# A written table of slots in place of computed positions, in an attention and expert layer

## The reference

```
xn = _layernorm(x)
x = x + attn(xn, ...) + ffn(xn, ...)

attn, for each of 16 heads of 16 numbers:
  scores = q k^T / 4                       # causal mask
  std    = softmax(scores) v Wo^T
  gsa    = softmax(scores + 0.3 * splat) v Wo^T   # splat: 16 features of q by 16 features of k
  attn   = (1 - blend) * std + blend * gsa

ffn, 16 experts, 2 for each token, room for 128 tokens in each:
  scores = sqrt(softplus(xn gate_w^T)); the two largest of scores + gate_b
  y      = sum over the two: w * W2[e] (silu(W1[e] xn) * (W3[e] xn))
  shared = Ws2 (silu(Ws1 xn) * (Ws3 xn))
```

## Time and profile before

| | |
|---|---|
| median of three runs | 359.38 us |
| lowest, highest | 357.64, 359.58 us |
| the profiled execution's own time | 357.81 us |
| its span, first to last instruction | 356.1 us |
| mean granted TensorE clock | 0.981 of 2.4 GHz |
| PE busy, share | 320.7 us, 90% |
| DVE busy, share | 237.0 us, 67% |
| ACT busy, share | 199.6 us, 56% |

### The profile page before, as it was taken

The page is one execution under the profiler, slowest core; times in us unless marked ns, Lnnn a source line. Parts: engine busy times, 40 slices in busy tenths (PEclk is TensorE's granted clock), DMA queues, the critical chain, the costliest instruction groups (busy, mean ns, idle before and its releaser), DMA issues.

```text
span 356.1 us, 6144 instructions
## 1 busy us (share of the span) xinstructions
PE 320.7 (90%) x2112; PEld 163.8 (46%) x2112; DVE 237.0 (67%) x693; ACT 199.6 (56%) x297; POOL 39.7 (11%) x59
## 2 busy tenths in 40 slices
PE   1989988987879999899999999999999999999984
PEld 1437733332433454444554454445445554445352
DVE  5988585497997668865676657755765568566424
ACT  1567457574635575754655564555556545647730
POOL 7200000000010000111111111102010004444000
PEclk9998999998987999999999999999999999999999
DMA  7423354324136502545465545454554443222011
GB/s 243 131 45 55 58 93 100 60 38 67 20 59 142 113 2 43 125 100 147 99 137 132 162 115 146 114 127 110 132 139 131 109 82 77 62 62 64 9 61 59
DMA packets 25823, 33.56 MB, mean 94 GB/s; under 512 B 4668, under 2 KB 18588, under 8 KB 25788
## 3 DMA queue, kind: packets, MB, share of 16 engines
q1 hardware_dynamic: 24088, 28.85, 35.6%
q0 software_dynamic: 1536, 4.20, 4.2%
q10 hardware_dynamic: 164, 0.07, 0.1%
HBM read 16.15 MB, written 4.26 MB: 57 GB/s over the span
## 4 chain that ended last, share of the span: by engine, by line
PE 45%; DVE 6%; ACT 3%; issue 2%; DVEq 0%
PE ps L914 12%; PE ps L830 7%; PE ps L839 5%; PE ps L896 5%; PE ps L884 4%; PE ps L790 4%; PE ps L869 2%; ACT arena_p L682 2%; PE ps L887 1%; DVE mx L1257 1%; PE ps L834 1%; ACT small L694 1%; PE ps L843 1%; DVE wt L1273 1%; DVE ps L1224 1%
## 5 line engine op out<-in xcount | busy, mean ns | idle before, releaser
L682 ACT ACTIVATE arena_p<-ps 128x1024 f32<-128x1024 f32 (+1 forms) x192 | 148.0, 808 | 52.0 <-PE ps L896 30.5
L1257 DVE TENSOR_REDUCE mx<-ps 128x1 f32<-128x512 f32 (+1 forms) x100 | 60.2, 628 | 20.8 <-PE ps L790 14.2
L914 PE MATMUL ps<-arena_p,v_full 128*32 128x512 f32 (+3 forms) x768 | 74.0, 504 | 0.0
L790 PE MATMUL ps<-stage 96*128 96x512 bf16 (+3 forms) x160 | 49.7, 347 | 7.5 <-DVE mx L1257 3.5
L884 PE MATMUL ps<-stage 98*128 98x512 bf16 (+1 forms) x192 | 51.3, 332 | 4.2 <-ACT arena_p L682 3.0
L896 PE MATMUL ps<-stage 98*128 98x512 bf16 (+1 forms) x192 | 46.8, 332 | 1.9 <-ACT arena_p L682 1.9
L456 POOL DMA_INDIRECT wt<-xn_scratch,ids_sb x16 | 15.3, 957 | 236.8 <-PE ps L818 103.6
L1224 DVE CUSTOM_DVE_ANT_0 ps<-ps,mask_r 128x128 f32<-128x128 f32 (+1 forms) x80 | 38.6, 498 | 2.6 <-PE ps L790 2.5
L914 PEld LDWEIGHTS ps<-arena_p,v_full 128*32 128x32 f32 x768 | 20.3, 110 | 34.9 <-issue 30.4
L790 PEld LDWEIGHTS ps<-stage 96*128 96x128 bf16 x160 | 15.5, 98 | 29.1 <-issue 21.2
L687 ACT ACTIVATE small<-ps 128x176 f32<-128x176 f32 x24 | 7.6, 317 | 37.1 <-PE ps L830 37.1
(11 more groups left out here) (204 smaller groups left out, 387.1 us busy)
## 6 DMA issues: line engine op xcount, KB each, us to landing
w_sb<-in_w_dram SPq DMA_DIRECT2D x16, 352.0 KB
stage<-split SPq DMA_DIRECT2D x48, 96.0 KB, 2.8
stage<-split SPq DMA_DIRECT2D x96, 32.0 KB, 2.3
stage<-split SPq DMA_DIRECT2D x48, 64.0 KB, 2.7
arena_o<-in_w_dram SPq DMA_DIRECT2D x16, 176.0 KB
ye_scratch<-wt SPq DMA_DIRECT2D x16, 128.0 KB, 2.3
stage<-split SPq DMA_DIRECT2D x32, 48.0 KB
acc<-in_x_dram SPq DMA_DIRECT2D x4, 256.0 KB, 3.7
```

The lines of the kernel that those rows point to most:

```text
L682: A(to, ps[:, 1 + 2 * s:3 + 2 * s, off:CH], ACT.Exp, scale=SCALE).then_inc(done, 1)
L790: ins = M(b[:, 0:n1 - n0], qs[0:KR, pr, h, it * P:(it + 1) * P], ks[0:KR, pr, h, n0:n1], start=True, stop=not masked)
L914: ins = M(ps[c:c + 2 * HD, 0, off:CH], v_full[:, jb + s, g * GH + h, :], of, start=jb + s == 0, stop=end or last, skip_group_check=last an ...
L1257: V.reduce_max(to, b[:, 0:n1 - n0], AX.X).then_inc(aux_free, 1)
```

## The change

The functions and lists that compute the positions go, and `PLAN` is written out: eight lists of 24 lists. Every task that stood in the lists before stands in them once; 166 of the 337 keep their slot. Nothing else is changed: what a task does, the waits, the banks' rotation, the fixed work and SP's rows. As banks go by the order of tasks, a task can now wait for another one than before. `AT` (the slot of each task that isn't repeated) is read off the table.

In the table groups differ from each other. Some of what changes:

- Group 0: all eight `pre` maxima stand in slots 0 to 2, both `square` in slot 4, `p0` 4 in slot 5 instead of 8, both `feat1` of the first column half in slot 6 and of the second in slot 10; the ten last maxima stand one by one or in threes between slots 12 and 19; `route` 3 follows `route` 2 in slot 14, `rest` 4 comes in from group 1, `rest` 5 likewise.
- Group 1: `route` 6 in slot 1 and `route` 7 in slot 6, one `max` each in slots 2 to 5, `oT` 1 in slot 7 instead of 3.
- Groups 2 to 5: `shift` 0 in slot 8 or 9, ahead of the maxima of the second half; `max` (0, 5, 1) in slot 10; `xT` of the expert that `gu` takes in slot 22 comes in slot 18 or 19 instead of 20; one maximum at slot 12, 16 and 20; `oT` 1 moves between slots 1 and 4.
- Groups 5 and 6: `hT` in slot 0, `y` in slot 1, `max` (0, 3, 0) only in slot 6 and 5; in group 6 five maxima stand in slot 5 and none in slots 6 and 7.
- Group 7: `out` (6, 0) in slot 9 instead of 10, `oT` 0 in 10 instead of 11, `rows` (1, 0) in 15 instead of 13, `out` (0, 2) in 18 instead of 16, `oTh` 0 in 23 instead of 21; `add` grouped.

The diff, cut:

```diff
-        def slotted(*lists):
-            slots = [[] for _ in range(NSLOT)]
...
-        def spread_late(tasks, first, last):
-            late_slots = [n for n in range(first, last + 1) if n % 4]
-            return [(late_slots[len(late_slots) * n // len(tasks)], t) for n, t in enumerate(tasks)]
...
-        SHARED = ((("sgu", 2), ("shT", 5), ("sy", 6)), (("sgu", 7), ("shT", 9), ("sy", 10)))
-        EXPERT = ((("xT", 0), ("gu", 2), ("hT", 5), ("y", 6)), (("xT", 5), ("gu", 7), ("hT", 9), ("y", 10)))
-
-        maxima = spread_late(max0, 0, 6) + [(9, ("shift", 0))] + spread_late(max1, 7, 20) + [(22, ("shift", 1))]
...
-        AT = {t: at for at, t in long}
-        PLAN = []
-        for g in range(NG):
-            lists = [[(11, ("oT", 0))], [(at - g * NSLOT, t) for at, t in long if at // NSLOT == g]]
...
+        PLAN = [
+            [
+                [("pre", ("max", (1, 4, 0))), ("pre", ("max", (1, 4, 1))), ("pre", ("max", (1, 5, 0))),
+                 ("pre", ("max", (1, 5, 1)))],
+                [("pre", ("max", (1, 6, 0))), ("pre", ("max", (1, 6, 1))), ("pre", ("max", (1, 7, 0)))],
+                [("pre", ("max", (1, 7, 1)))],
+                [("max2", (0,))],
+                [("square", 0), ("square", 1), ("pre", ("shift", 1))],
+                [("max2", (1,)), ("p0", 4), ("max", (0, 2, 0))],
+                [("feat1", (0, 1)), ("feat1", (1, 1)), ("max", (0, 3, 0))],
+                [("max", (1, 2, 0))],
+                [("max", (1, 3, 0)), ("route", 0)],
+                [("p0", 5)],
+                [("max", (0, 4, 0)), ("feat1", (0, 0)), ("feat1", (1, 0)), ("max", (0, 4, 1)), ("max", (0, 5, 0)),
+                 ("max", (0, 5, 1))],
+                [("route", 1), ("oT", 0)],
+                [("shift", 0), ("max", (0, 6, 0))],
+                [("max", (0, 6, 1)), ("max", (0, 7, 0)), ("max", (0, 7, 1)), ("max", (1, 4, 0))],
+                [("max", (1, 4, 1)), ("route", 2), ("route", 3)],
+                [],
+                [],
+                [("max", (1, 5, 0)), ("max", (1, 5, 1)), ("max", (1, 6, 0))],
+                [("max", (1, 6, 1))],
+                [("max", (1, 7, 0)), ("max", (1, 7, 1)), ("rest", 4)],
+                [("route", 4)],
+                [],
+                [("shift", 1)],
+                [("route", 5), ("rest", 5)],
+            ],
+            [
+                [],
+                [("max2", (0,)), ("max2", (1,)), ("route", 6)],
+                [("max", (0, 2, 0)), ("p1", 4)],
+                [("max", (0, 3, 0))],
+                [("max", (1, 2, 0))],
+                [("max", (1, 3, 0))],
+                [("route", 7), ("p1", 5)],
+                [("max", (0, 4, 0)), ("oT", 1)],
...
+                [("max2", (0,)), ("max2", (1,))],
+                [("rest", 6), ("shT", 2), ("rest", 7), ("sy", 2)],
+                [("max", (0, 2, 0))],
+                [("sgu", 3), ("oT", 1), ("max", (0, 3, 0))],
...
+                [("hT", 2), ("xT", 3), ("oT", 1)],
+                [("y", 2), ("max2", (0,))],
+                [("gu", 3), ("max2", (1,)), ("max", (0, 2, 0))],
+                [("hT", 3), ("max", (0, 3, 0))],
+                [("max", (1, 2, 0)), ("max", (1, 3, 0))],
+                [("y", 3)],
+                [("max", (0, 4, 0)), ("max", (0, 4, 1))],
+                [("shift", 0)],
+                [("xT", 4), ("max", (0, 5, 0))],
+                [("max", (0, 5, 1)), ("max", (0, 6, 0))],
+                [("oT", 0), ("gu", 4), ("max", (0, 6, 1))],
+                [("max", (0, 7, 0)), ("max", (0, 7, 1))],
+                [("hT", 4)],
+                [("xT", 5), ("y", 4), ("max", (1, 4, 0)), ("max", (1, 4, 1))],
+                [("gu", 5), ("max", (1, 5, 0))],
+                [("max", (1, 5, 1))],
+                [("hT", 5), ("max", (1, 6, 0))],
+                [("y", 5), ("xT", 6), ("max", (1, 6, 1))],
+                [("max", (1, 7, 0))],
+                [("max", (1, 7, 1))],
+                [],
+                [("gu", 6)],
+                [("shift", 1)],
...
+                [("hT", 10)],
+                [("xT", 11), ("max2", (0,)), ("y", 10), ("max2", (1,)), ("max", (0, 2, 0))],
+                [],
+                [("oT", 1), ("gu", 11)],
+                [],
+                [],
+                [("hT", 11), ("max", (0, 3, 0)), ("max", (1, 2, 0))],
+                [("max", (1, 3, 0)), ("max", (0, 4, 0)), ("y", 11)],
+                [("max", (0, 4, 1)), ("shift", 0), ("max", (0, 5, 0)), ("xT", 12)],
+                [("max", (0, 5, 1)), ("max", (0, 6, 0)), ("max", (0, 6, 1))],
...
+                [("gu", 15), ("oT", 1)],
+                [("hT", 15), ("sgu", 4), ("y", 15)],
+                [("max", (0, 3, 0)), ("max", (1, 2, 0)), ("max", (1, 3, 0)), ("max", (0, 4, 0)), ("max", (0, 4, 1))],
+                [],
+                [],
+                [("shift", 0), ("shT", 4)],
...
+                [("add", (0, 5)), ("out", (4, 0)), ("add", (1, 5))],
+                [],
+                [],
+                [("out", (6, 0))],
+                [("oT", 0)],
+                [],
+                [("add", (0, 6))],
+                [("add", (1, 6)), ("add", (0, 7)), ("add", (1, 7))],
+                [],
+                [("rows", (1, 0))],
+                [],
+                [],
+                [("out", (0, 2))],
+                [("out", (2, 2))],
+                [],
+                [],
+                [],
+                [("oTh", 0)],
+            ],
+        ]
+        AT = {t: g * NSLOT + n for g, slots in enumerate(PLAN) for n, tasks in enumerate(slots) for t in tasks
+              if t[0] not in ("max2", "max", "shift", "pre", "oT")}
```

More of the change, by code:

```diff
@@ L260, in bass_splat_attention_moe_layer @@
-        maxima = spread_late(max0, 0, 6) + [(9, ("shift", 0))] + spread_late(max1, 7, 20) + [(22, ("shift", 1))]
-        LATER = 8
[L262 to L271, removed]
+        LATER = 8
@@ L272, in bass_splat_attention_moe_layer @@
         LAST_FEAT = ("feat1", (1, 0))
-        S_ROUTE, S_SHARED, S_EXPERT, S_ADD = (8, 31), (32, 148), 56, 156
         OWN_AT = (0, 3)
[L275 to L281, removed]
```

124 lines of the change are left out of this document (112 added, 12 removed).

## The result

The changed kernel takes 343.65 us (343.28 to 344.06, four runs) against 358.51 us, the median of the kernel before with a fourth run beside the three. That is a ratio of 0.9585, 95% interval 0.9548 to 0.9622. Forecast were 348.4 us. The profiled execution took 343.76 us with a span of 342.0 us, 14.1 us under the span before.

A forecast was written before the change was run, and what follows sets the result against it. PE was taken as the bound (busy 90%), DVE through group 0 and the start of group 1. Terms -4.5 - 1.0 - 6.0 + 0 - 1.0 + 2.0 = -10.5 us from 357.81, plus 1.1: 348.4 us; range 343 to 354, 356.5 with the DVE case.

The forecast's parts named there:

- Group 0 and the start of group 1, -4.5 us: Group 0 and first third of group 1: DVE's idle time falls from 9.1 to 4.6 us, bounds 0 to -9.1.
- the clock, -1.0 us: Groups 0 and 1: part of the cost of running at 1.2 GHz goes, -1.0 us, bounds +3.4 to -3.4.
- the second stretch: Group 1: 6.8 us at half clock, costing at most 3.4 us; two thirds of that cost was kept.
- Groups 2 to 5, -6.0 us: PE's six short waits mostly go: -1.0, -1.8, -2.2 and -1.0 us by group, bounds 0 to -10.4.
- Group 6, 0: Five maxima in slot 5 cost about 1.3 us, as much as goes at slots 9, 15, 19 and 22; net 0.
- Group 7, -1.0 us: out (0, 2) behind both splats fills the wait of std (5, 0), 0.95 us; rounded -1.0, bounds 0 to -1.5.
- What I can't see, +2.0 us: Groups 1 to 7: new unseen waits, 0.3 us in each of seven groups, +2.0 us, bounds 0 to +8.
- SP, 0: Ahead of max2: slack shrinks about 0.4 us, costed at nothing; rival of late rows, 1 us per group, 352 us, chance 0.08.
- DVE giving the gain back: Rival, first 50 us: DVE's fixed load returns the gain; 353 us, up to 357; chance 0.18.
- The slower side: Clock rival, groups 1, 2, 5, 6: bursts of maxima bring more half-clock stretches, 3.4 us each; 366 us; chance 0.08.
- The sum: Whole kernel: terms add to -10.5 us, 347.3 us; with 1.1 us from profiled execution to the runs, 348.4 us.
- The signs: Group 3 about 2 us shorter, group 0 4 to 5, DVE idle about half, std (5, 0) wait gone, one half-clock stretch in group 1.

The follow-up runs named there:

- a burst: The changed kernel with four maxima of group 0 moved from slots 17 and 18 to slot 15; 350.60 us, ratio 0.9772.
- early maxima: Against the kernel where group 5 was refilled as well: max (0, 3, 0) and max (0, 4, 1) ahead of feat1 in group 0; 340.16 us, ratio 0.9464.
- the third set: Runs on one chip of the kernel where group 5 was refilled as well and three edits of it, beside the kernel before, median 359.9 us.
- the run that shows it alone: The changed kernel with computed slots for groups 5 and 6, the table for 0 to 4 and 7; 341.56 us, ratio 0.9543.
- group 5 was refilled as well: Previous run, but group 5 takes the table's group 4 slots, group 6 maxima, shift and oT as in its group 3; 339.05 us, ratio 0.9473.
- the first kernel: The kernel before with the table for groups 0 and 1 only, computed slots for 2 to 7; 348.83 us, ratio 0.9750.

## Why the prediction was right, and where it was off

The direction and its reasons held, and the time lies in the range; the forecast was 4.7 us too high. By its own steps:

- **Group 0 and the start of group 1, -4.5 us, and the clock, -1.0 us.** Measured -9.3 us for groups 0 and 1. The rule behind the first term is that DVE's idle time counts. Three kernels show it: with a burst, with early maxima and with the table in the middle groups only, group 0 grew by 6.2, 1.7 and 1.3 us where DVE's idle time grew by 6.2, 2.0 and 1.3 us. In the changed kernel it fell from 9.8 to 4.7 us, where 4.6 were worked out; the sum had started from the four longest waits, 9.1 us, and so was 0.7 us short. The step that was mis-sized is the clock. I kept two thirds of the second stretch, since new waits of 2.9 and 1.7 us were to come. They came, as 1.8 and 1.1 us, and where the clock fell with them (the table for groups 0 and 1 alone) it cost nothing, since DVE was busy meanwhile. What the clock took before can be estimated from the kernel before itself: seven of its runs in the third set had a mean clock of 0.971 and a mean of 360.1 us, two had 0.981 and 357.5. A hundredth of 356 us of lost clock is 3.6 us, that is 7.1 us at half speed, for 2.6 us of time, 0.37 us for each. The 10.2 us at half clock in the loop then were worth some 3.8 us, an estimate from these runs, and about 5.5 us were waits. No run has the computed slots of groups 0 and 1 at full clock, so this division isn't shown, nor which moves in group 0 brought its part. One wait of DVE in the second stretch, just behind the window of the earlier trace rows, is gone in the changed kernel:

```profile
108.94 0.69 DVE L1323 COPY pv_sb<-ps 128x512 f32<-128x512 f32 x1 [1.60 <-PE ps L914]
```

- **Groups 2 to 5, -6.0 us.** Measured -2.2 - 1.9 - 2.5 + 0.5 = -6.1 us, by the parts -1.0, -1.8, -2.2, -1.0. For group 5 I was 1.5 us too hopeful: I had seen its wait in slot 8 (0.44 us printed, 0.60 really), not those of `shift` 1 and `std` (6, 0, 0), which stand behind `gu` 14 in slot 21 and start 0.40 and 0.58 us late. For group 2 I was 1.2 us too careful: `oT` 1 didn't wait for the two `rest`s. The slots that I named for groups 2 to 5 are those of groups 3 and 4: in group 5 `max` (0, 5, 1) stands in slot 9, and slots 10 and 12 differ too. The two misses cancel, so it is partly luck that the whole term came out.
- **Group 6, 0.** +1.4 us. The five maxima cost about what was worked out (some 1.1 us by their starts, 276.17 to 278.12 us, the longest wait 0.45 us; 1.3 us were forecast), but `sy` 4 in slot 9 waits another 1.0 us, behind them on DVE, and ACT is late three times.
- **Group 7, -1.0 us.** 1.0 us in the run that shows it alone. The row of `std` (5, 0) has no wait: `splat`s, `out`, `std` follow one another.

```profile
325.18 0.93 PE L1055 MATMUL ps<-stage 98*128 98x512 bf16 x4
325.95 1.89 PE L1028 MATMUL ps<-wt,rest 128*128 128x256 f32 x8
327.68 0.28 PE L1043 MATMUL ps<-stage 98*128 98x256 bf16 x1
```

- **What I can't see, +2.0 us.** Not there in groups 1 to 4, where the measured gains need no such term; in groups 5 and 6 it was, as 2.9 us. Spread over all groups it was the wrong shape: unseen waits stood where the table was dense.
- **SP, 0.** No wait in the changed kernel. Once group 5 was refilled as well, the first showed, with 0.16 us printed.
- **The rivals.** DVE giving the gain back fell with the first kernel: group 2 was 37.7 us long there, as before the change. The slower side fell too: behind group 1 no profiled run shows the half clock, except behind the last matmul of PE. (Its sum comes to 366.5 us, and half of the 10.5 us is 5.3, not 6.) The Trainium skill, "TensorE: Matmul & The Clock Gate", section "A second HAM failure mode: psum-queue depth-cycling", names cycling through PSUM banks as a cause. Six short waits in group 3 before and those between the maxima in group 6 after, of up to 0.45 us, left the clock at 1.00, so here the short waits alone didn't bring it down.
- **The sum.** The span fell by 14.1 us where 10.5 were forecast. The other 1.1 us of the miss is the step from the profiled execution to the median: the changed kernel needed none (343.76 and 343.65 us). The time lies 0.7 us inside the range, near its end.
- **The signs.** The six waits of group 3, the 0.79 us ahead of `std` (5, 0) and half of DVE's idle time went. Group 0 lost 5.6 us, more than the 4 to 5. The one stretch of half clock in group 1 isn't in this profiled execution, but in that of the same slots in the first kernel of the first set.

## What to carry to other kernels

Where two engines run in order and hand work to each other, ask of each stretch which of them has the queue, and price a new order by what it takes off the idle time of that one; a wait of the other moved about here and cost nothing by itself. Before a task is moved, look at three places: the task three banks ahead of it, the engine that must serve it in between its own deadlines, and the place where it stood, and check each group by itself: a table that is better in six groups can be worse in two, and their slots can simply be filled from a good one.

## What the runs showed of the hardware

The granted clock differed from run to run of one kernel: in the third set the kernel before had a mean clock of 0.971, 0.976, 0.981 or 0.984, and times of 360.1, 359.3, 357.5 and 356.4 us (the first the mean of seven runs, the third of two). PE was busy by the profile for nearly all of each of three stretches of 3.4 us at half clock, and yet their cost differed. In two kernels it was 1.3 us, in group 0, where DVE was busy for 2.44 and 3.09 us of the stretch. It was nothing in group 1, where DVE was busy for 3.30 us of it: the group took 35.3 us with the stretch and 35.4 us without.
